# Moving the second batch's scaling layer into the first batch's wide attention

## The chip, the cores and the metric

The kernel runs on one core of one Trainium2 chip. The metric is the device time of one execution in microseconds, median over runs. Five engines work side by side from their own instruction queues and meet through semaphores: TensorE (PE) multiplies, VectorE (DVE) and ScalarE (ACT) do elementwise work, GpSimd (POOL) does elementwise work and issues indirect DMAs, and SyncE (SP) issues the other DMAs.

## The reference

An activation x of 2 batches x 512 tokens x 256 features goes through twelve sublayers, each a layer norm, a block and a residual sum. The last four matter here:

```python
x = x + 0.5 * _L2_ffn_ref(_layernorm(x, axis=-1), ...)   # second routed FFN: top 2 of 8 experts and a shared FFN
x = x + 0.5 * _L3_ffn_ref(_layernorm(x, axis=-1), L3_ffn_weight, L3_ffn_bias)   # scaling layer
x = x + _L3_attn_ref(_layernorm(x, axis=-1), L3_attn_W_Q, ..., L3_attn_W_O)     # wide attention
x = x + 0.5 * _L3_ffn_ref(_layernorm(x, axis=-1), L3_ffn_weight, L3_ffn_bias)
```

The scaling layer multiplies the normed x by a 256 x 256 matrix quantized to -1, 0 and 1 and adds a bias. The wide attention has 16 causal heads of 128 features over each batch.

## The kernel before, in words

Each sublayer of each batch is a unit: unit u is sublayer u // 2 of batch u % 2. Units 16 and 17 are the second routed FFN (MOE2), 18 and 19 the first scaling layer (FFN3), 20 and 21 the wide attention (ATT3), 22 and 23 the second scaling layer. Every engine walks the units in order by a program written out by hand. PE_OF, ACT_OF and DVE_OF name each engine's function for a unit, and SP and POOL have their own lists at the end of the file.

Products keep nearly full precision by splitting each operand into a high part (written by ACT or POOL) and a low part (the difference, written by DVE or POOL), and by three matmuls for one (mm3, lines 282 to 284). So each result that feeds a product passes through ACT and then DVE before PE can use it.

A layer norm is a chain over four engines: dve_stats (four bn_stats, four bn_aggr, small tensor_scalars), pool_ln (a power for the inverse root; for the units in NORM_ACT a second small product), the norm itself on DVE (dve_norm) or, for the units in NORM_ACT, on ACT (act_norm), pe_T (eight transposes into two PSUM banks), act_T and dve_T (high and low part of the transposed x).

The routed FFN handles both batches in one loop of 30 tiles (15 of each batch). SP loads tiles of gathered tokens into raw (m_xs) and stores results in DRAM; POOL gathers each token's two result rows back by eight indirect DMAs of a batch (pool_gather_y) into four slots in raw (m_gath), and DVE adds them to x (dve_combine, two instructions for each of four token tiles). Batch 0 is combined while batch 1's tiles are still multiplied. Batch 1 (unit 17) can only be gathered once its last tile is stored; its combination stands in dve_ffn3(18).

The order of the stretch that the change touches is this. PE ends the tile loop, multiplies the scaling layer of batch 0 (unit 18), waits for the transposed norm of batch 1, multiplies its scaling layer (unit 19), transposes the norm of unit 20, and begins ATT3 of batch 0 with queries and keys of its first head. DVE adds bias and product of unit 18, combines unit 17 as its gathers land, and then does statistics and norm of unit 19 and of unit 20. POOL gathers, does the small powers, and splits the first pair of heads' weights (pre(20)), which SP loads after unit 17 is done, since raw is shared.

In ATT3 the heads go in pairs. The first and the last pair are written out and the pairs between are a loop. For each head PE fills queries and keys of the next head (ACT copies, DVE takes the low part), transposes the probabilities, multiplies the scores of the next head, the probabilities by the values, and the output product. DVE takes the row minima of the scores (dve_min, L1779), ACT the exponential (L1787), DVE the reciprocal of the sums (dve_rinv, L1796), and POOL multiplies the probabilities by it (pool_norm, L1805). POOL also splits the next pair's weights (pool_chunks, L474 and L476). In before, the statistics of unit 21 stand in DVE's queue after the first head of ATT3 of batch 0.

Of the kernel before, what the change touches and what calls it, by code (L numbers as in the profile page):

```python
# [33 lines left out]
P = 128  # L34
NB = 2
# [76 lines left out]
def build(nc, a, out, stop=N_UNITS):  # L112

    with ExitStack() as ctx:
# [110 lines left out]
        _a, m_b = sublayer_tensors(_m_pad2=([P, 12000], F32), m_b=([P, E * EW], F32R))  # L225
        m_dl = small[:, 32:96].rearrange("p (b i e) -> p b i e", b=NB, i=TT)
# [88 lines left out]

        def dve_stats(v, u, tiles=range(TT)):
# [8 lines left out]
            for i in tiles:  # L325
                v.bn_stats(stats[:, b, i, :], x[:, TT * b + i, :]).then_inc(sem("ln_stats"), 1)  # L326
            if tiles[-1] < TT - 1:
                return
            for i in range(TT):
                v.wait_ge(sem("ln_stats"), TT * u + i + 1)  # L330
                v.bn_aggr(mv[:, b, i, :], stats[:, b, i, :]).then_inc(sem("ln_aggr"), 1)
            v.wait_ge(sem("ln_aggr"), TT * (u + 1))
# [4 lines left out]
        NORM_ACT = (1, 2, 3, 4, 5, 6, 7, 8, 11, 12, 13, 17)  # L337

        def act_norm(s, u):
# [4 lines left out]
            if u >= 2:  # L344
                s.wait_ge(sem("ln_T"), 2 * (u - 1))
# [4 lines left out]
        def dve_norm(v, u, tiles=range(TT)):  # L350
# [5 lines left out]
            if u not in NORM_ACT:  # L356
                v.wait_ge(sem("ln_rstd"), u + 1)
                if positive(2 * (u - 1)):
                    v.wait_ge(sem("ln_T"), 2 * (u - 1))
# [25 lines left out]
        def pool_ln(g, u):  # L385
# [4 lines left out]
            g.wait_ge(sem("ln_veps"), u + 1)  # L390
            g.tensor_tensor(rstd[:, b, :], veps[:, b, :], nhalf[:, :], ALU.pow).then_inc(sem("ln_rstd"), 1)  # L391
            if u in NORM_ACT:
                g.wait_ge(sem("ln_rstd"), u + 1)
# [3 lines left out]
        def T_bank(u):  # L397

            return 2 if u in (14, 18) else 0

        def pe_T(pe, u):
# [4 lines left out]
            pe.wait_ge(sem("ln_xn"), TT * (u + 1))  # L406
            if positive(2 * u):
                pe.wait_ge(sem("ln_lo"), 2 * u)
# [9 lines left out]
        def act_T(s, u):  # L418
# [3 lines left out]
            for c in range(DC):  # L422
                s.wait_ge(sem("ln_T"), 2 * u + c + 1)
# [7 lines left out]
        def dve_T(v, u):  # L431
# [3 lines left out]
            for c in range(DC):  # L435
                v.wait_ge(sem("ln_hi"), 2 * u + c + 1)
# [8 lines left out]
        def pe_ready(pe, u):  # L445

            pe.wait_ge(sem("ln_lo"), 2 * (u + 1))
# [345 lines left out]
        def pe_moe2(pe, u):  # L793
# [131 lines left out]
            for n in range(n0 - 1, n0 + N2 + 2):  # L925
# [10 lines left out]
                if n0 <= n - 1 < n0 + N2:  # L936
                    tile_h(n - 1)
                if n0 <= n - 2:
# [85 lines left out]
        def dve_combine(v, u, part):  # L1024

            b, m = u % 2, MOE2_AT[u] // 2
            for k in range(2):
                a_ = 2 * part + k
                v.wait_ge(sem(f"m_got{a_ % 4}"), 16 * (2 * (2 * m + b) + a_ // 4 + 1))
# [3 lines left out]
                ins = v.scalar_tensor_tensor(out=xt, in0=m_gath[:, a_ % 4, :], scalar=m_w[:, b, part, k:k + 1], in1=xt,  # L1033
# [193 lines left out]
        def pool_gather_y(g, u, half):  # L1227
# [40 lines left out]
        def sp_moe2(sp, u):  # L1268
# [303 lines left out]
        def act_T_next(s, u):  # L1572
            act_T(s, u + 1)


        def pe_ffn3(pe, u):
            b, m = u % 2, F3_AT[u]
# [4 lines left out]
            else:  # L1582
                units_done(pe, u)
# [8 lines left out]
            pe_T(pe, u + 1)  # L1592

        def dve_ffn3(v, u):
            b, m = u % 2, F3_AT[u]

            def bias():
                v.wait_ge(sem("const_in"), 16 * CONSTS)
                for t in range(TT):
                    xt = x[:, TT * b + t, :]  # L1600
                    v.scalar_tensor_tensor(out=xt, in0=bias3[:, :], scalar=0.5, in1=xt, op0=ALU.mult, op1=ALU.add)\
                        .then_inc(sem("f3_bias"), 1)

            def residual():
                v.wait_ge(*since("f3_bias", 4 * (m + 1)))
                dve_residual(v, u, 0.5, [("f3_out", 2 * m + 1), ("f3_out", 2 * m + 2)])

            if u == 18:
                bias()
                residual()  # L1610
                for t in range(TT):
# [1218 lines left out]
```

## Time and profile before

| what | us |
|---|---|
| median of 3 runs | 1260.48 (1258.39 to 1263.32) |
| the profiled execution's own time | 1263.04 |
| its span in the trace | 1261.2 |
| mean granted TensorE clock | 0.94 of full speed |
| busy: PE, DVE, ACT, POOL | 1091.8, 849.2, 609.0, 558.2 |

The span is what the trace shows from the first instruction to the last; 1.8 us lie around it. A granted clock of 1.00 is 2.4 GHz and 0.50 is 1.2 GHz. Times of rows are microseconds from the start of the span.

### The profile page before, as it was taken

The page shows a single profiled execution, that of the slowest core. Times are in us where ns is not written, and L with a number is a line of the kernel's source. Part 1 is how long each engine was busy: PE and PEld are TensorE (multiplying, and loading weights), DVE is VectorE, ACT ScalarE, POOL GpSimd, SP SyncE. Part 2 cuts the span into 40 slices and gives each one's busy share as a digit, 9 for nine tenths or more (in the row PEclk, how much of TensorE's full clock was granted, in tenths as well). Part 3 has the DMA queues.
Part 4 walks back from the last instruction along what each step waited for, and adds up shares of the span by engine and source line. Part 5 has one row for each costly group of instructions (what it writes and reads, how often), then busy time and mean ns, then how long its engine had stood idle before and what let it go on. Part 6 is the DMA issues. An engine that isn't in the chain of part 4 may idle for free.

```text
span 1261.2 us, 21660 instructions
## 1 busy us (share of the span) xinstructions
PE 1091.8 (87%) x6545; PEld 936.6 (74%) x6545; DVE 849.2 (67%) x2302; ACT 609.0 (48%) x1434; POOL 558.2 (44%) x666
## 2 busy tenths in 40 slices
PE   5887478999779989988989998992899998999995
PEld 4776367778557779867767777981799997899995
DVE  4577766778977756668768876565656565665666
ACT  2455734321114345567758754550455554555552
POOL 5576618750345440254524438124344442444430
PEclk9898879999889999989989997995899998999998
DMA  5125212230013033322512123432101010010100
GB/s 171 63 66 219 87 68 83 77 113 10 1 62 120 1 114 116 115 76 66 161 34 46 24 80 101 125 112 69 44 26 50 25 50 26 26 50 25 48 2 34
DMA packets 48450, 87.85 MB, mean 70 GB/s; under 512 B 9648, under 2 KB 28464, under 8 KB 47920
## 3 DMA queue, kind: packets, MB, share of 16 engines
q1 hardware_dynamic: 41232, 70.17, 17.5%
q0 software_dynamic: 5120, 13.83, 3.6%
q10 hardware_dynamic: 2016, 2.83, 0.6%
q8 instruction: 43, 0.70, 0.2%
q14 instruction: 39, 0.32, 0.1%
HBM read 61.24 MB, written 19.27 MB: 64 GB/s over the span
## 4 chain that ended last, share of the span: by engine, by line
PE 59%; DVE 21%; ACT 9%; issue 7%; POOL 3%; DMA 1%; SPq 0%; DVEq 0%; another core or an unknown queue 0%; POOLq 0%; ACTq 0%
PE ps L282 18%; PE ps L283 16%; PE ps L284 16%; PE ps L1818 4%; DVE a_ptl L1842 3%; DVE a_p L1779 2%; ACT a_p L1787 2%; ACT a_pth L1834 1%; PE ps L415 1%; DVE x L1560 1%; PE ps L856 1%; DVE stats L326 1%; DVE ffn_hf L726 1%; PE ps L875 1%; DVE ffn_hl L730 1%
## 5 line engine op out<-in xcount | busy, mean ns | idle before, releaser
L1805 POOL TENSOR_SCALAR a_p<-a_p,small 128x128 f32<-128x128 f32 (+3 forms) x256 | 132.6, 537 | 233.5 <-DVE small L1796 233.3
L1787 ACT ACTIVATE a_p<-a_p,small 128x128 f32<-128x128 f32 (+3 forms) x256 | 141.5, 554 | 74.6 <-DVE small L1779 72.4
L1842 DVE TENSOR_TENSOR a_ptl<-ps,a_pth 128x384 fp32r<-128x384 f32 (+1 forms) x192 | 106.6, 596 | 62.7 <-ACT a_pth L1834 62.2
L282 PE MATMUL ps<-xh,wh 128*128 128x512 f32 x304 | 126.3, 416 | 10.1 <-POOL wl L507 5.8
L283 PE MATMUL ps<-xl,wh 128*128 128x512 f32 x304 | 122.8, 404 | 0.0
L284 PE MATMUL ps<-xh,wl 128*128 128x512 f32 x304 | 122.4, 403 | 0.0
L1834 ACT ACTIVATE a_pth<-ps 128x384 fp32r<-128x384 f32 (+1 forms) x192 | 90.4, 523 | 57.6 <-PE ps L1818 57.5
L1779 DVE CUSTOM_DVE_ANT_0 a_p<-ps,maskrow 128x128 f32<-128x128 f32 (+3 forms) x256 | 111.6, 483 | 5.0 <-PE ps L284 2.1
L391 POOL TENSOR_TENSOR rstd<-veps,nhalf 128x4 f32<-128x4 f32 x24 | 25.2, 1051 | 160.8 <-DVE veps L335 160.8
L476 POOL TENSOR_TENSOR wl<-raw,wh 128x1024 fp32r<-128x1024 f32 (+1 forms) x66 | 91.9, 1392 | 5.5
L1818 PE MATMUL ps<-ident,a_p 128*128 128x128 f32 x640 | 86.6, 284 | 8.3 <-POOL a_p L1805 4.2
L282 PE MATMUL ps<-m_a,xh 128*128 x240 | 84.1, 350 | 4.8 <-DVE xl L1157 1.7
L474 POOL TENSOR_SCALAR wh<-raw 128x1024 fp32r<-128x1024 f32 (+1 forms) x66 | 46.7, 708 | 82.5 <-PE ps L284 82.3
L1818 PEld LDWEIGHTS ps<-ident,a_p 128*128 128x128 f32 x640 | 73.7, 146 | 11.4 <-POOL a_p L1805 5.5
L282 PEld LDWEIGHTS ps<-xh,wh 128*128 128x128 f32 x304 | 59.0, 194 | 25.4 <-POOL wl L507 7.7
L283 PE MATMUL ps<-m_b,xh 128*128 x240 | 73.3, 305 | 0.0
L284 PE MATMUL ps<-m_a,xl 128*128 x240 | 73.2, 305 | 0.0
L1238 POOL DMA_INDIRECT raw<-moe_y,m_pos x32 | 31.6, 986 | 91.1 <-DMA moe_y<-m_y 65.6
L415 PE MATMUL ps<-ident,xn 128*128 128x128 f32 x176 | 27.8, 310 | 49.2 <-issue 31.6
L284 PEld LDWEIGHTS ps<-xh,wl 128*128 128x128 f32 x304 | 58.8, 193 | 14.5
L1560 DVE SCALAR_TENSOR_TENSOR x<-ps,small,x 128x256 f32<-128x256 f32 x128 | 61.7, 482 | 8.6 <-PE ps L284 2.2
L283 PEld LDWEIGHTS ps<-xl,wh 128*128 128x128 f32 x304 | 58.9, 194 | 10.9
(368 smaller groups left out, 3438.3 us busy)
## 6 DMA issues: line engine op xcount, KB each, us to landing
raw<-in_w SPq DMA_DIRECT2D x32, 384.0 KB
raw<-in_qk SPq DMA_DIRECT2D x16, 512.0 KB
raw<-moe_x SPq DMA_DIRECT2D x60, 128.0 KB
moe_y<-m_y SPq DMA_DIRECT2D x60, 128.0 KB
m_raw<-in_ex SPq DMA_DIRECT2D x8, 608.0 KB, 7.7
m_raw<-in_ex POOLq DMA_DIRECT2D x8, 608.0 KB, 4.2
raw<-in_v SPq DMA_DIRECT2D x16, 256.0 KB
moe_x<-drh SPq DMA_DIRECT2D x8, 480.0 KB
```

The source lines that it names most:

```text
L282: pe.matmul(o, l[0], r[0], start=start, stop=False, skip_group_check=True)
L283: pe.matmul(o, l[0], r[1], start=False, stop=False, skip_group_check=True)
L284: return pe.matmul(o, l[1], r[0], start=False, stop=stop, skip_group_check=True)
L474: g.tensor_scalar(oh, raw[:, p, at:n], 1.0, 1.0, ALU.mult, ALU.mult).then_inc(sem("w_hi"), 1)
L476: g.tensor_tensor(ol, raw[:, p, at:n], f32(oh), ALU.subtract).then_inc(sem("w_split"), 1)
L1560: v.scalar_tensor_tensor(out=xt, in0=ps[:, 2 + t, e * D:(e + 1) * D], scalar=w_moe1[:, t, 2 * k + e:2 * k + e + 1], in1=xt, op0=ALU.mult, ...
L1779: v.tensor_tensor_reduce(p[:, par, P_AT[i]:P_AT[i + 1]], ps[:, bank, at:at + KEYS[i]], maskrow[:, T - KEYS[i]:T], 1.0, -NEG, ALU.add, ALU.min,
L1787: s.activation(p[:, par, P_AT[i]:P_AT[i + 1]], p[:, par, P_AT[i]:P_AT[i + 1]], ACT.Exp, bias=h_nmx[:, par, i:i + 1], scale=scale, accum_ou ...
L1805: g.tensor_scalar(pp, pp, h_inv[:, par, i:i + 1], 1.0, ALU.mult, ALU.mult).then_inc(sem("at_norm"), 1)
L1818: last = pe.transpose(ps[:, banks[f], at:at + P], p[:, par, P_AT[i] + kb * P:P_AT[i] + (kb + 1) * P], ident[:, :])
L1834: s.activation(dst, ps[:, bank, 0:cols], func, **how).then_inc(sem("at_fhi"), 1)
L1842: ins = v.tensor_tensor(dst, ps[:, bank, 0:cols], f32(hi), ALU.subtract)
```

## The change

- Unit 18's product (now pe_scale3(18)) goes into the tile loop of the routed FFN, ahead of the last tile's down product. ATT3 of batch 0 comes next: transposes, ACT copy and DVE low part of unit 20 stand where unit 19's stood. Unit 20's norm moves from DVE to ACT, and so does unit 19's.
- Unit 17's gathers get a buffer of their own (m_late, eight slots), with no wait for slots; they come after unit 20's small powers in POOL's queue. Its combination stands in the first pair of ATT3 on DVE: tiles 0 and 1 between minima and reciprocal of the first head, tiles 2 and 3 around the next head's query split.
- Unit 19 (statistics, powers, norm, transposes, split, bias, product, residual) goes into the first pair of ATT3, with its transposes in banks 6 and 7. The first head's output product moves behind it, and the statistics of unit 21 move one head later.
- The first pair's weights are loaded by SP inside the routed FFN's loop, before its last two stores; the high part is written by ACT and the low part by DVE in place of POOL.
- The semaphore counts of the layer norms follow the new order (LN_AT). The final store of batch 1 is cut into two halves.

The core of the diff:

```diff
+        LN_AT = {u: u for u in range(N_UNITS)} | {20: 19, 19: 20}
-        NORM_ACT = (1, 2, 3, 4, 5, 6, 7, 8, 11, 12, 13, 17)
+        NORM_ACT = (1, 2, 3, 4, 5, 6, 7, 8, 11, 12, 13, 17, 20, 19)
...
+                if m == 1 and n == n0 + N2 + 1:
+                    pe_scale3(pe, 18)
                 if n0 <= n - 2:
                     tile_down(n - 2, at.pop(n - 2))
...
-                if 2 * TT * q + c >= 4:
+                if u < 17 and 2 * TT * q + c >= 4:
                     g.wait_ge(*since("m_comb", 2 * TT * q + c - 3))
-                g.indirect_dma_start(out=m_gath[:, c % 4, :], out_offset=None, in_=ys[b][:, :],
+                g.indirect_dma_start(out=m_late[:, c, :] if u == 17 else m_gath[:, c % 4, :], out_offset=None, in_=ys[b][:, :],
...
+                if m == 1 and n == n0 + N2:
+                    sp.wait_ge(*since("t_x", n0 + N2))
+                    sp.wait_ge(sem("x_res0"), 4 * 9)
+                    sp.wait_ge(*since("sh_lo", SH_CH * 2 * NB))
+                    for p in range(2):
+                        sp_chunks(sp, 20, 0, p)
...
+        def act_ffn3(s, u):
+            if u == 18:
+                for p in range(2):
+                    n, r = chunk_cols(20, p), RAW0[20] + p
+                    s.wait_ge(sem(f"w_raw{p}"), 16 * (RAW0[20] // 2) + 16)
+                    s.activation(wh[:, p, 0:n], raw[:, p, 0:n], ACT.Copy).then_inc(sem("w_hi"), 1)
+                act_norm(s, 20)
+                act_T(s, 20)
...
         def dve_ffn3(v, u):
             if u == 18:
+                dve_bias3(v, 18)
+                dve_residual3(v, 18)
+                dve_stats(v, 20)
+                for p in range(2):
+                    n = chunk_cols(20, p)
+                    v.wait_ge(sem("w_hi"), RAW0[20] + p + 1)
+                    v.tensor_tensor(wl[:, p, 0:n], raw[:, p, 0:n], f32(wh[:, p, 0:n]), ALU.subtract)\
+                        .then_inc(sem("w_split"), 1)
+                dve_T(v, 20)
...
@@ pe_att3, first pair @@
+                    if side and first and hh == 1:
+                        pe_T(pe, side)
                     pe_transpose_p(pe, n + hh, hh, a3_p, [bank["p", hh, f] for f in range(3)],
                                    [starts["p", hh, f] for f in range(3)])
+                    if side and first and hh == 1:
+                        pe_scale3(pe, side)
                     if not done:
                         scores(n + (hh + 1), at["k", hh, 0] + 1)
+                    if side and first and hh == 1:
+                        units_done(pe, u)
+                        out_head(0, at["z", 0, 0] + 1, start=True)
...
@@ act_att3, first pair @@
+                    if u in SIDE and first and hh == 1:
+                        act_T(s, SIDE[u])
...
+                    if u in SIDE and first and hh == 0:
+                        act_norm(s, SIDE[u])
...
@@ dve_att3 @@
+                    if side and first and hh == 0:
+                        dve_combine(v, 17, 2)
                     if not done:
                         one(("q", hh, 0), a3_ql[:, :], a3_qh[:, :], scale=-SCALE3)
+                    if side and first and hh == 0:
+                        dve_combine(v, 17, 3)
+                    if not done:
                         one(("k", hh, 0), a3_kl[:, :], a3_kh[:, :])
+                    if side and first and hh == 1:
+                        dve_bias3(v, side)
+                        dve_T(v, side)
...
+                    if side and first and hh == 1:
+                        dve_residual3(v, side)
                     if not done:
                         dve_min(v, n + (hh + 1), 1 - hh, a3_p)
+                        if side and first and hh == 0:
+                            dve_stats(v, side)
                         dve_rinv(v, n + (hh + 1), 1 - hh)
                     one(("z", hh, 0), a3_zl[:, :], a3_zh[:, :])
-                    if first and hh == 0:
+                    if first and hh == (1 if side else 0):
                         dve_stats(v, u + 1)
...
             dve_min(v, n0, 0, a3_p)
+            if side:
+                dve_combine(v, 17, 0)
+                dve_combine(v, 17, 1)
             dve_rinv(v, n0, 0)
...
@@ pool_att3, first pair @@
                     if not last:
                         pool_chunks(g, u, r + 1, hh)
+                    if u in SIDE and first and hh == 0:
+                        pool_ln(g, SIDE[u])
...
-            for b in range(NB):
-                sp.wait_ge(sem(f"x_res{b}"), 4 * N_UNITS // 2)
+            for b, t, n in ((0, 0, TT), (1, 0, 2), (1, 2, 2)):
+                sp.wait_ge(sem(f"x_res{b}"), 4 * N_UNITS // 2 - TT + t + n)
...
@@ gpsimd @@
             pool_moe2(g, 16)
+            pool_ln(g, 20)
             pool_gather_y(g, 17, 0)
             pool_gather_y(g, 17, 1)
-            pool_ln(g, 19)
-            pool_ln(g, 20)
-            g.wait_ge(*since("sh_down", SH_CH * 2 * NB))
-            pre(20)
             pool_att3(g, 20)
```

## Rows read from the trace of the kernel before

**Rows 1.** The chain that ended last, 848 to 887 us: start, us, what

```profile
848.30 0.38 PE ps L282
...
850.45 2.14 PE ps L1588 x16
852.59 18.46 issue
...
878.18 4.85 issue
883.03 1.96 PE ps L415 x8
...
886.39 0.80 PE ps L282
```

**Rows 2.** Busy time in windows: PE, PEld, DVE, ACT, POOL, granted clock, DMA share, GB/s

```profile
852.60:858.00 5.40, 0.00 (x0) 0.00 (x0) 1.24 (x3) 0.00 (x0) 3.02 (x4) 0.82 0.17 50
...
890.00:892.00 2.00, 1.17 (x5) 0.65 (x3) 0.84 (x2) 0.77 (x2) 0.00 (x0) 0.95 0.00 0
```

**Rows 3.** DVE in order of time, 848 to 896 us: start, us, instruction

```profile
848.41 1.42 DVE L1601 SCALAR_TENSOR_TENSOR x<-bias,x 128x256 f32<-128x256 f32 x4
851.76 1.62 DVE L459 SCALAR_TENSOR_TENSOR x<-ps,x 128x256 f32<-128x256 f32 x4 [1.94 <-PE ps L1588]
...
874.26 1.40 DVE L326 BATCH_NORM_STATS2 stats<-x 128x6 f32<-128x256 f32 x4
...
895.42 0.08 DVE L1779 DVE_READ_ACCUMULATOR2_ANT small<- 128x1 f32 x1
```

**Rows 4.** POOL in order of time, 854 to 904 us

```profile
854.07 1.01 POOL L1238 DMA_INDIRECT raw<-moe_y,m_pos  x1 [12.17 <-issue]
...
862.96 0.96 POOL L1238 DMA_INDIRECT raw<-moe_y,m_pos  x1 [0.30 <-issue]
...
876.29 1.05 POOL L391 TENSOR_TENSOR rstd<-veps,nhalf 128x4 f32<-128x4 f32 x1 [6.76 <-DVE veps L335]
...
900.49 1.05 POOL L474 TENSOR_SCALAR wh<-raw 128x1024 fp32r<-128x1024 f32 x1 [2.26 <-PE ps L284]
901.62 2.39 POOL L476 TENSOR_TENSOR wl<-raw,wh 128x1024 fp32r<-128x1024 f32 x1
```

**Rows 5.** POOL and ACT in order of time around unit 17's norm

```profile
735.27 0.20 POOL L395 TENSOR_TENSOR nmr<-negm,rstd 128x4 f32<-128x4 f32 x1
...
739.51 2.06 ACT L347 ACTIVATE xn<-x,nmr,rstd 128x256 f32<-128x256 f32 x4
```

**Rows 6.** The experts' weight splits on ACT and DVE: ns min/median/max, first and last start

```profile
L767 ACT ACTIVATE m_a<-m_raw x16: 1199/1202/1222, 383.3 to 759.9; 128x1216 fp32r<-128x1216 f32 x16
...
L772 DVE TENSOR_TENSOR m_b<-m_raw,m_a x8: 1403/1406/1407, 750.1 to 768.4; 128x1216 fp32r<-128x1216 f32 x8
```

**Rows 7.** SP's first weight load of unit 20

```profile
866.77 0.35 SPq L466 DMA_DIRECT2D raw<-in_qk  x1
```

**Rows 8.** The window in which both its pieces were moved, columns as in Rows 2

```profile
868.00:870.00 2.00, 0.00 (x0) 0.00 (x0) 0.74 (x6) 0.00 (x0) 1.04 (x1) 0.50 0.88 341
```

**Rows 9.** PE in order of time, first pair of ATT3, batch 0

```profile
901.81 0.55 PE L1818 MATMUL ps<-ident,a_p 128*128 128x128 f32 x3 [0.65 <-DVE a_kl L1842]
...
915.73 0.33 PE L282 MATMUL ps<-wh,xh 128*128 128x256 f32 x1
```

**Rows 10.** Lines whose DVE instructions read two SBUF tiles: ns min/median/max

```profile
L1723 DVE SCALAR_TENSOR_TENSOR lin_xn<-lin_kv,small x8: 476/710/954, 332.1 to 357.4; 128x256 f32<-128x256 f32 x8
...
L730 DVE TENSOR_TENSOR ffn_hl<-ffn_hf,ffn_hh x32: 691/695/2878, 21.5 to 256.1; 128x512 fp32r<-128x512 f32 x32
```

**Rows 11.** Two windows of PE gaps late in the span, columns as in Rows 2

```profile
1057.00:1058.00 1.00, 1.00 (x9) 1.00 (x8) 0.00 (x0) 0.00 (x0) 0.92 (x2) 0.73 0.00 0
...
1234.00:1236.00 2.00, 0.01 (x1) 0.02 (x1) 1.03 (x3) 1.21 (x4) 1.68 (x4) 1.00 0.00 0
```

**Rows 12.** The final stores, by line

```profile
DMA to landing us min/median/max: 2.9/2.9/2.9
```

More of the change, by code:

```diff
@@ L397, in T_bank @@
         def T_bank(u):
-            return 2 if u in (14, 18) else 0
+            return {14: 2, 18: 2, 19: 6}.get(u, 0)
         def pe_T(pe, u):
@@ L1032, in dve_combine @@
                 xt = x[:, TT * b + part, :]
-                ins = v.scalar_tensor_tensor(out=xt, in0=m_gath[:, a_ % 4, :], scalar=m_w[:, b, part, k:k + 1], in1=xt,
+                ins = v.scalar_tensor_tensor(out=xt, in0=m_late[:, a_, :] if late else m_gath[:, a_ % 4, :], scalar=m_w[:, b, part, k:k + 1], in1=xt,
                                              op0=ALU.mult, op1=ALU.add)
@@ L1591, in pe_ffn3 @@
                     last.then_inc(sem("f3_out"), 1)
-            pe_T(pe, u + 1)
-        def dve_ffn3(v, u):
[L1595 to L1606, printed above, removed]
-            if u == 18:
-                bias()
-                residual()
-                for t in range(TT):
-                    dve_combine(v, 17, t)
+        def pe_ffn3(pe, u):
+            if u == 18:
+                pe_T(pe, 20)
+            if u >= 22:
+                pe_ready(pe, u)
+                units_done(pe, u)
+                pe_scale3(pe, u)
+                pe_T(pe, u + 1)
@@ new lines, in act_ffn3, with dve_bias3 @@
+        def act_ffn3(s, u):
+            if u == 18:
+                for p in range(2):
[4 more added lines that the diff above has]
+                act_T(s, 20)
+            if u == 22:
+                act_T(s, 23)
+        def dve_bias3(v, u):
+            v.wait_ge(sem("const_in"), 16 * CONSTS)
+            for t in range(TT):
+                xt = x[:, TT * (u % 2) + t, :]
+                v.scalar_tensor_tensor(out=xt, in0=bias3[:, :], scalar=0.5, in1=xt, op0=ALU.mult, op1=ALU.add)\
+                    .then_inc(sem("f3_bias"), 1)
@@ L2118, in pair @@
                         qk(1 - hh, [bank["q", hh, 0], bank["k", hh, 0]], [starts["q", hh, 0], starts["k", hh, 0]])
-                    if first and hh == 0:
+                    if side and first and hh == 1:
+                        pe_T(pe, side)
+                    if first and hh == 0 and not side:
                         units_done(pe, u)
-                    else:
+                    if not first or (hh == 1 and not side):
                         out_head(r * 2 + (hh - 1), (base if hh == 0 else at["z", 0, 0] + 1), start=first)
@@ L2148, in act_att3, with pair @@
             b, n0, f0 = u % 2, A3_HEADS[u], A3_FILL[u]
-            def pair(r, last=False):
+            def pair(r, last=False, first=False):
                 fills = pair_fills(last)
@@ L2173, in act_att3 @@
             act_exp(s, n0, 0, -1.0, a3_p)
-            pair(0)
+            pair(0, first=True)
             with s.Fori(1, H // 2 - 1) as r:
@@ L2586, in chunks @@
             def chunks(u):
[L2587 removed]
+                with sp.Fori(1 if u in (0, 20) else 0, CHUNKS[KIND[u]] // 2) as i:
                     for p in range(2):
```

68 lines of the change are left out of this document (35 added, 33 removed).

## The prediction

> **What bounds the kernel now.** I read the chain that ended last first. Between the routed FFN and the wide attention it shows 18.46 us in which PE waits for nothing on its own account, and 4.85 us more after unit 19's product [rows 1]. The timelines of DVE and POOL name what runs meanwhile: gathers of unit 17 one after the other from 854.07, their combination, then unit 19's whole norm, then unit 20's, whose statistics begin at 874.26 [rows 3, 4]. PE's transposes for unit 20 begin at 883.03 and the attention's first product at 886.39 [rows 1]. The windows show PE idle and its granted clock falling on the way; it is back near full only in 890 to 892 [rows 2]. In the attention itself PE is the chain's engine, so time is won by starting it earlier and lost by what is put into it.
>
> **Part 1: the start of the attention.** Unit 18's product takes the place of the last down product. It can start when the down product before has issued: that one starts at 848.30 and is six matmuls of about 0.12, so at 849.0 and not at 850.45 [rows 1], 1.45 earlier. DVE's residual ended at 851.76 + 1.62 = 853.38 behind it [rows 3]; now 851.93. Statistics to the end of the power took 876.29 + 1.05 - 874.26 = 3.08 [rows 3, 4]. The second product on POOL adds its 0.20 [rows 5] and some 0.16 of gaps and one DVE instruction: 855.4. Beside the power DVE splits the low weights. ACT and DVE need 1.20 and 1.40 us for 1216 columns [rows 6], so by width 1.0 and 1.2 for 1024 and about 0.6 and 0.7 for 512. Whether a long DVE instruction holds back POOL's power is not in the trace: nothing, or both pieces (1.9); I take 0.6, since the power's row is of its usual length next to four bias instructions. So 856.0; four ACT norms take 2.06 [rows 5]: transposes start at 858.1, and everything up to the first product keeps its distance, as PE has again been idle and I count on the same low clock. The shift is 858.1 - 883.03 = **-24.9**.
>
> The weights don't delay this. SP loads them after the store of the third last tile, whose down product ends before the one at 848.30 [rows 1]: about 848.1. The two pieces were loaded before from 866.77, and the DMA engines were 0.88 busy in 868 to 870 [rows 7, 8], so they land about 3.4 us later, at 851.5; ACT is free when it has copied the last tile (849.0 + 1.9 for unit 18, 0.7 for the down product, 0.5 for the copy: 852.1) and done with both by 853.7. If they landed as late as 7 us after issue, ACT's norm would still not wait by more than 1. The last two stores go behind these loads in SP's queue and the last down product is 1.9 later, so the gathers start near 856, behind unit 20's power, at (862.96 - 854.07) / 7 = 1.27 apart [rows 4] (eight, 10.2 us). Their last lands about 868. DVE wants the first four at 895.5 - 24.9 = 870.6 (the last minimum ends at 895.5 [rows 3]). POOL is free for the first pool_norm as well. Cost 0, with some 7 us of slack for the first four; beyond that DVE's reciprocal, and behind it POOL, PE and ACT, would wait microsecond for microsecond.
>
> **Part 2: the work put into the first pair**, on the clock of before (subtract 24.9 for the new one). Eight combining instructions at about 0.55 with their waits are 4.4 us on DVE. The first four move the reciprocal from 895.9 to 897.7 and POOL's norm to 900.0, when PE comes to transpose anyway (900.2): free. The other four stand around the query split; without any hindrance the low part of the keys ends at 902.9 and not 901.8, **+1.15** on PE, which waits for just that [rows 9].
>
> But POOL splits the next weights there: 1.05 us from 900.49 and 2.39 from 901.62 [rows 4], and combining reads two SBUF tiles. Two lines of that kind stretch beside POOL's work: 476 to 954 ns and 691 to 2878 ns [rows 10]. So one instruction can lose nothing or up to 2.19. I place the four in time: one behind POOL's last norm (0.6), one or two behind POOL's two pieces. The low keys then end at 906.2, **+3.3** more; bounds 0 and 4.
>
> From there PE's third transpose group runs at 906.2. Scores until 908.6, minima until 909.8. Statistics of unit 19 (1.95) come before the reciprocal; then POOL's two small products (1.4) to 913.2, ahead of POOL's norm of the second head; ACT's norm of unit 19 (2.06) to 915.3, ahead of ACT's copies of queries and keys. PE transposes unit 19 (1.1); ACT copies queries and keys (1.1), DVE takes the low parts by 917.2, adds the bias (1.6 with a short wait) and splits unit 19 (1.3) to 920.1. PE's product takes 1.9, scores 2.0, first output product 1.5, values 1.85: the second pair starts at 927.3. Before it was 915.73 [rows 9]. From the third transposes on that is 21.1 us in place of 13.9, **+7.1**. Of this only 3.0 is PE's own work; the rest is ACT standing before unit 19's norm, and DVE between statistics and split. The statistics of unit 21, one head later, fit into POOL's and DVE's slack: their row cost DVE 2 us in before as well, and POOL's norm in the second pair ends some 0.6 before PE wants it.
>
> **The clock.** In before, PE's clock stayed full in this pair. Now PE has some 5 us with only a few transposes, then two gaps of over 2 us. Late in the span one gap of 2.0 us was followed by a fall to 1.2 GHz (0.73 in 1057 to 1058) and another was not [rows 11]. A fall costs until PE has worked on for a while; from 886.39 to about 890 in before [rows 1, 2], so some 2 us of full-clock work is doubled. I take **+2.3**, bounds 0 and 5.
>
> **Tail.** The last store is halved. It landed in 2.9 us [rows 12]; half the bytes at the 341 GB/s of [rows 8] save 0.7 at most. I take **-0.5**, bounds 0 and -0.8.
>
> **Sum:** -24.9 + 1.15 + 3.3 + 7.1 + 2.3 - 0.5 = -11.5. On the profiled execution's own 1263.04 that is 1251.5. That execution lies 2.6 above the median of the runs, 1260.48; from the median, **1249.0**.
>
> **A rule against the change.** POOL's pieces are the point: [rows 10] give 0.24 for the middle row of the shorter line and 2.19 for the worst of the longer, so four combining instructions would cost 1.0 by the first. The Trainium skill (SBUF — State Buffer, section "Who interferes with whom") says that a VectorE instruction with two SBUF inputs and a GpSimd one that reads SBUF exclude each other, the later waiting for the whole of the earlier. The longest row bears that out, the shortest doesn't tell. By the middle row the sum would be -13.8, by the rule the -11.5 above, and the same rule would let the low-weight split hold back unit 20's power.
>
> **Rivals.**
> - *Power behind the split*: both DVE pieces (1.2 and 0.7) run before POOL's power on the way to the start, 1.3 more than I took: 1250.3. For it: two SBUF inputs on DVE [rows 10]; against it: the power's row at its usual 1.05 [rows 4].
> - *Blocked, but the clock holds*: -13.8, 1246.7. For it: the window at 1234 [rows 11]; against it: the wider gap.
> - *No block*: combining slips between POOL's pieces, PE has no wide gap and the clock holds: -24.9 + 1.15 + 6.8 - 0.5 = -17.5, 1243.0. For it: the shortest times in [rows 10]; against it: POOL's pieces start just there.
> - *The attention doesn't start earlier in effect*: gathers land late and hold the first reciprocal. From 7 us of lateness each microsecond counts; at 12 more the gain is gone, 1255 to 1260. Against it: 1.27 per gather, nothing else in POOL's queue.
> - *Slower*: the granted clock stays at 1.2 GHz through the pair, because its gaps return before PE has worked long enough. Each us of full-clock work done low costs one. Beyond the 2.3 counted, 13.8 us cancel the gain, and 20 make it slower by over 0.5%: 1267. The first pair holds some 26 us of PE work. Against it: every fall in these rows ended after a few us of work [rows 2].
>
> **Chances.** Forecast 0.43; power behind the split 0.08; blocked with full clock 0.16; no block 0.24; late gathers 0.05; low clock throughout 0.04. Anything under 0.5% (6.3 us) can't be told from no change here: below 1254.2 is faster. The first four cases are, but for the forecast's upper end (I give 0.02 of it to no change); late gathers count as no change, the low clock as slower by 0.03 and else as no change. So faster 0.89, no change 0.08, slower 0.03. The range takes the no-block case and a bit of its unused bound (a smaller +6.8), and above it the late power with a second fall of the clock: 1241.5 to 1253.5.
>
> **What the next profile would show.** Transposes of unit 20 some 25 us earlier than 883; if not, the ACT norm or the weights are late, and ACT's row before its high split names which. In the first pair, combining rows stretched beyond 0.48 us or a POOL piece beyond 2.39 for the block; a DVE idle entry on a gather for the late gathers; the granted clock in 1 us windows for the fall. First product to second pair 29.3 us in before, about 43 by my sum, 37 without the block. Wrong would be a pair of under 34 or over 47.

## The result and the profile after

| what | before | after |
|---|---|---|
| median of the runs of one job, us | 1261.53 (4 runs, 1258.39 to 1263.32) | 1248.84 (4 runs, 1246.65 to 1253.06) |
| ratio, 95% interval | | 0.990 [0.988, 0.992] |
| profiled execution: own time, span | 1263.04, 1261.2 | 1253.06, 1251.3 |
| mean granted clock | 0.940 | 0.942 |

Three of the later runs hold one execution in a slow state (2070.19, 1331.33 and 5751.22 us), which is left out of their medians and ratios.

The forecast was 1249.0. How it came out is told best by distances from one mark that both kernels reach by the same code: the start of unit 18's transposes. It lies at 845.25 in the kernel before and at 850.14 in the changed one. In a second profile of the changed kernel (the control, next section) it lies at 845.14, so these 5 us differ from execution to execution and have nothing to do with the change. Rows of PE, kernel before:

```profile
845.25 0.30 PE L415 MATMUL ps<-ident,xn 128*128 128x128 f32 x1
1064.65 0.30 PE L415 MATMUL ps<-ident,xn 128*128 128x128 f32 x1
```

The same of the changed kernel, with the landmarks of the first pair between (unit 20's transposes, first product of the attention, third transposes, unit 19's transposes, second pair); a bracket is the idle time ahead and what ended it. They answer to [rows 1, 9]:

```profile
850.14 0.30 PE L419 MATMUL ps<-ident,xn 128*128 128x128 f32 x1
...
863.48 1.94 PE L419 MATMUL ps<-ident,xn 128*128 128x128 f32 x8 [6.72 <-ACT xn L351]
866.83 0.79 PE L283 MATMUL ps<-xh,wh 128*128 128x512 f32 x1 [1.41 <-DVE xl L447]
...
886.29 0.90 PE L1846 MATMUL ps<-ident,a_p 128*128 128x128 f32 x3 [3.16 <-DVE a_kl L1870]
897.00 1.07 PE L419 MATMUL ps<-ident,xn 128*128 128x128 f32 x8 [1.12 <-issue]
908.52 0.34 PE L283 MATMUL ps<-wh,xh 128*128 128x256 f32 x1
...
1055.31 0.30 PE L419 MATMUL ps<-ident,xn 128*128 128x128 f32 x1
```

Start of each landmark less that of unit 18's transposes in the same profile, us; the runs below are described in the next section:

| profile | unit 20's transposes | first product | unit 19's transposes | second pair | unit 21's transposes | end of span |
|---|---|---|---|---|---|---|
| before | 37.78 | 41.14 | 25.80 | 70.48 | 219.40 | 415.95 |
| after | 13.34 | 16.69 | 46.86 | 58.38 | 205.17 | 401.16 |
| control | 13.35 | 16.70 | 46.91 | 58.39 | 205.13 | 401.06 |
| split after combining | 13.34 | 16.69 | 44.61 | 57.65 | 205.31 | 402.89 |
| bridge in the first pair | 13.33 | 16.69 | 44.93 | 56.41 | 205.35 | 401.24 |
| split by GpSimd | 12.51 | 15.86 | 46.89 | 58.40 | 205.11 | 402.54 |
| before, bridged | 37.86 | 41.21 | 25.89 | 70.44 | 217.12 | 414.27 |
| power first | 13.53 | 16.89 | 46.44 | 57.96 | 204.70 | 400.72 |
| all bridged | 13.34 | 16.69 | 45.08 | 56.61 | 203.37 | 399.61 |
| block, clock, power | 13.55 | 16.90 | 42.89 | 53.56 | 200.25 | 396.73 |
| waits only | 12.51 | 15.86 | 42.42 | 52.98 | 199.71 | 395.62 |
| the same, five bridges | 12.50 | 15.86 | 42.33 | 52.99 | 199.71 | 395.82 |
| eight bridges | 12.38 | 14.99 | 39.12 | 49.77 | 196.51 | 390.87 |

From the mark to the end the change took off 415.95 - 401.16 = 14.8 us: 24.45 won at the start of the attention, 12.35 given back in the first pair (29.3 us from the first product to the second pair before, 41.7 now), 2.1 won between the second pair and unit 21's transposes (148.9 to 146.8), and 0.6 won behind that.

POOL and DVE in order of time say what holds the start, and what holds the first pair; they answer to [rows 3, 4]:

```profile
858.99 1.85 POOL L395 TENSOR_TENSOR rstd<-veps,nhalf 128x4 f32<-128x4 f32 x1 [12.18 <-DVE veps L339]
860.91 0.20 POOL L399 TENSOR_TENSOR nmr<-negm,rstd 128x4 f32<-128x4 f32 x1
...
870.45 0.95 POOL L1245 DMA_INDIRECT m_late<-moe_y,m_pos  x1 [0.30 <-issue]
879.16 2.25 POOL L1833 TENSOR_SCALAR a_p<-a_p,small 128x128 f32<-128x128 f32 x4 [7.76 <-DVE small L1824]
881.50 1.08 POOL L478 TENSOR_SCALAR wh<-raw 128x1024 fp32r<-128x1024 f32 x1
882.66 2.45 POOL L480 TENSOR_TENSOR wl<-raw,wh 128x1024 fp32r<-128x1024 f32 x1
```

```profile
858.75 1.82 DVE L1640 TENSOR_TENSOR wl<-raw,wh 128x1024 fp32r<-128x1024 f32 x2
...
876.08 2.30 DVE L1040 SCALAR_TENSOR_TENSOR x<-m_late,small,x 128x256 f32<-128x256 f32 x4
...
880.20 1.47 DVE L1040 SCALAR_TENSOR_TENSOR x<-m_late,small,x 128x256 f32<-128x256 f32 x2
...
882.44 2.96 DVE L1040 SCALAR_TENSOR_TENSOR x<-m_late,small,x 128x256 f32<-128x256 f32 x2
885.54 0.69 DVE L1870 TENSOR_TENSOR a_kl<-ps,a_kh 128x512 fp32r<-128x512 f32 x1
```

The power takes 1.85 us beside the low split and 1.05 in [rows 4]; that the split holds it back is tested below. Combining takes 0.58 us an instruction where POOL is idle (2.30 for four). The last two take 2.96 together, and 2.38 of that is the second of them alone: it starts at 883.01, behind POOL's second weight piece, and ends at 885.39, just after that piece (885.11). The low part of the keys, for which PE idles 3.16 us, stands right behind them. The last gather is issued at 870.45 and no DVE row waits for it. The windows (columns as in [rows 2], the clock third from the end) show the price of that idle time, and a place where the clock now stays up, at the hand-over between the two attentions:

```profile
884.00:886.00 2.00, 0.00 (x0) 0.00 (x0) 1.85 (x2) 0.00 (x0) 1.11 (x1) 0.69 0.00 0
886.00:888.00 2.00, 1.71 (x8) 1.72 (x9) 1.55 (x4) 0.49 (x1) 0.00 (x0) 0.50 0.75 246
888.00:890.00 2.00, 2.00 (x8) 1.89 (x7) 1.49 (x7) 0.82 (x4) 0.00 (x0) 0.50 0.07 25
890.00:892.00 2.00, 2.00 (x7) 1.59 (x6) 1.29 (x6) 1.30 (x5) 0.00 (x0) 0.60 0.00 0
...
1052.00:1054.00 2.00, 1.16 (x7) 1.03 (x8) 1.20 (x3) 0.94 (x3) 1.92 (x3) 1.00 0.00 0
```

PE idles for 2.0 us ahead of that place in either kernel (first row before, second row changed):

```profile
1056.45 0.38 PE L282 MATMUL ps<-drh,a_zh 128*128 128x256 f32 x1 [2.01 <-DVE a_zl L1842]
1049.29 0.39 PE L283 MATMUL ps<-drh,a_zh 128*128 128x256 f32 x1 [2.02 <-DVE a_zl L1870]
```

The windows of the kernel before, where the fall began in [rows 11]:

```profile
1059.00:1061.00 2.00, 1.23 (x6) 0.83 (x6) 0.91 (x2) 1.09 (x2) 1.92 (x3) 0.50 0.00 0
1061.00:1063.00 2.00, 2.00 (x7) 1.71 (x8) 0.80 (x2) 0.49 (x1) 1.27 (x1) 0.50 0.68 231
```

### The profile page after: what moved, and what is told of

It reads as the page before. It is cut to its first block, busy times and chain, and to the rows that moved or that the text cites. A ratio compares the mean times of both kernels' runs of the same rounds, so it can differ in the third digit from the quotient of the medians.

```text
span 1251.3 us, 21657 instructions
## 1 busy us (share of the span) xinstructions
PE 1097.6 (88%) x6545; PEld 941.7 (75%) x6545; DVE 845.9 (68%) x2298; ACT 616.0 (49%) x1444; POOL 556.7 (44%) x664
## 4 chain that ended last, share of the span: by engine, by line
PE 54%; DVE 17%; ACT 6%; issue 4%; POOL 3%; DMA 1%; SPq 0%; DVEq 0%; POOLq 0%; ACTq 0%
PE ps L283 16%; PE ps L285 15%; PE ps L284 15%; PE ps L1846 4%; DVE a_ptl L1870 3%; DVE a_p L1807 2%; ACT a_p L1815 2%; ACT a_pth L1862 2%; DVE x L1573 1%; PE ps L860 1%; PE ps L879 1%; DVE stats L329 1%; PE ps L419 1%; POOL raw L1245 1%; PE ps L1595 1%
## 5 line engine op out<-in xcount | busy, mean ns | idle before, releaser
L283 PE MATMUL ps<-xh,wh 128*128 128x512 f32 x304 | 127.1, 418 | 10.5 <-POOL wl L511 6.0
L480 POOL TENSOR_TENSOR wl<-raw,wh 128x256 fp32r<-128x256 f32 (+1 forms) x64 | 88.3, 1380 | 5.3
L1846 PEld LDWEIGHTS ps<-ident,a_p 128*128 128x128 f32 x640 | 72.9, 145 | 14.9 <-POOL a_p L1833 6.0
L478 POOL TENSOR_SCALAR wh<-raw 128x256 fp32r<-128x256 f32 (+1 forms) x64 | 45.7, 713 | 78.5 <-PE ps L285 78.2
L285 PEld LDWEIGHTS ps<-xh,wl 128*128 128x128 f32 x304 | 59.0, 194 | 14.6
L283 PE MATMUL ps<-drh,xh 128*128 (+2 forms) x160 | 61.0, 381 | 2.2 <-DVE x L1573 2.2
L285 PE MATMUL ps<-drh,xl 128*128 (+2 forms) x160 | 59.7, 373 | 0.0
```

The lines of the kernel that those rows point to most:

```text
L283: pe.matmul(o, l[0], r[0], start=start, stop=False, skip_group_check=True)
L285: return pe.matmul(o, l[1], r[0], start=False, stop=stop, skip_group_check=True)
L478: g.tensor_scalar(oh, raw[:, p, at:n], 1.0, 1.0, ALU.mult, ALU.mult).then_inc(sem("w_hi"), 1)
L480: g.tensor_tensor(ol, raw[:, p, at:n], f32(oh), ALU.subtract).then_inc(sem("w_split"), 1)
L1846: last = pe.transpose(ps[:, banks[f], at:at + P], p[:, par, P_AT[i] + kb * P:P_AT[i] + (kb + 1) * P], ident[:, :])
```

## The experiments

Medians are of the runs of one job and go with the ratio to the kernel before in that job; the chips of the jobs differ by some us, so jobs are compared by ratios. Small differences are read from the table of landmarks. In the expectations "unit 19's low keys" are the low part of the second head's keys, which PE waits for ahead of unit 19's work, and where the run with the power first speaks of unit 19's transposes as the mark, unit 18's are meant.

**Control: the changed kernel again.**

> The changed kernel as it is, beside which the others of this job are read. Both theories: about 1249 us, about 0.990 of the kernel before; from the end of unit 19's low keys to the second pair a clock of 0.50 for some 5 us.

1248.42 us, ratio 0.989 [0.987, 0.991]; every landmark within 0.1 us of the first profile. The gain from mark to end, 14.9 us, repeats, and this execution has none of the 5 us ahead of the mark.

**GpSimd's split after the combining.**

```diff
@@ pool_att3, first pair, before pool_chunks @@
+                    if u in SIDE and first and hh == 0:
+                        g.wait_ge(*since("m_comb", 8 * TT))
```

> GpSimd's first chunk of the next pair's weight split, inside the first pair of the second attention, waits until the last VectorE product of the combining is done; nothing else changes. Theory (GpSimd's split of 2.45 us holds back the combining's two-input products, and so unit 19 behind them): the product that took 2.96 us takes about 0.7, unit 19's low keys are ready about 2.3 us earlier after unit 20's first product (17.1 instead of 19.4 us), and the time falls by 2.3 to 3 us against the changed kernel, by up to 2 more if the shorter idle time keeps TensorE's clock from falling. Rival (no block: the products are late for another reason): the product keeps its 2.9 us and the time stays within 0.5 us. Second rival (the split, now later, makes the second pair's weights late): the time rises by 1 us or more, and the second pair's first matmul waits for the split.

1247.61 us, ratio 0.987 [0.985, 0.989]. DVE and POOL:

```profile
878.38 1.06 DVE L1040 SCALAR_TENSOR_TENSOR x<-m_late,small,x 128x256 f32<-128x256 f32 x2
879.59 0.69 DVE L1870 TENSOR_TENSOR a_kl<-ps,a_kh 128x512 fp32r<-128x512 f32 x1
```

```profile
879.53 1.05 POOL L478 TENSOR_SCALAR wh<-raw 128x1024 fp32r<-128x1024 f32 x1 [2.18 <-DVE x L1040]
```

The two take 1.06 and not 2.96 us: the block is real, and the row is 1.9 longer for it. The third transposes come 17.9 us behind the first product and not 19.5; the other 0.4 went ahead of the combining, where PE's clock came back 5.1 us behind the first product and not 4.4. Unit 19's transposes come 2.3 us earlier, since the clock still falls behind the key split but is back after some 3 us and not 7. But only 0.7 of that reaches the second pair: the clock falls again in front of unit 19's product, and once more, as briefly, at the hand-over. PE doesn't wait for the later weight split at the second pair. The time can't be told from the control's. The windows behind the key split and in front of unit 19's product:

```profile
881.00:883.00 2.00, 2.00 (x10) 1.90 (x10) 1.66 (x7) 0.83 (x4) 2.00 (x1) 0.54 0.00 0
883.00:885.00 2.00, 2.00 (x7) 1.60 (x6) 1.29 (x5) 1.37 (x6) 0.04 (x1) 0.60 0.45 70
...
894.00:896.00 2.00, 1.36 (x7) 1.36 (x8) 2.00 (x4) 0.00 (x0) 0.00 (x0) 0.71 0.18 69
896.00:898.00 2.00, 2.00 (x11) 2.00 (x11) 0.86 (x3) 0.00 (x0) 0.00 (x0) 0.50 0.00 0
```

**A bridge over the idle time in the first pair.** Transposes whose result nobody reads.

```diff
@@ pe_transpose_p, behind the second group of the first head @@
+                if isinstance(n, int) and n == A3_HEADS[20] and f == 1:
+                    pe.wait_ge(sem("x_res0"), 4 * 10)
+                    for _ in range(24):
+                        pe.transpose(ps[:, 6, 0:P], ident[:, :], ident[:, :])
```

> 24 transposes of the identity, whose results nobody reads, are added on TensorE behind the second group of transposes of the first head, where it idled for about 3.2 us before unit 19's low keys; the rest of the work is the same. Theory (the fall of the granted clock to 0.50 behind that idle time costs 2.3 us of the 42 us from unit 20's first product to the second pair): the clock stays at 1.00 or near it from the third transposes on and the time falls by about 2 us. Rival (the slower matmuls there are hidden by waits for VectorE and ScalarE): the clock stays high as well, but the stretch keeps its 42 us and the time is within 0.7 us of the changed kernel.

1248.75 us, ratio 0.989 [0.987, 0.991]. The clock stays at 1.00 through the pair and the second pair starts 2.0 us earlier, as the theory says. Unit 21's transposes do not: at the hand-over, where the control has 1.00, this profile has

```profile
1044.00:1046.00 2.00, 1.61 (x8) 1.21 (x6) 0.36 (x1) 0.95 (x2) 2.00 (x2) 0.50 0.00 0
```

and from the second pair to unit 21's transposes it needs 148.9 us, just what the kernel before needed, and not 146.7. So both of my statements were too simple: the fall costs 2.0 us where it is, and a second fall took them back.

**The first pair's weights split by GpSimd again.** Placed behind unit 20's small products; ACT's and DVE's loops are gone.

```diff
@@ gpsimd @@
             pool_ln(g, 20)
+            g.wait_ge(*since("sh_down", SH_CH * 2 * NB))
+            pre(20)
             pool_gather_y(g, 17, 0)
```

> The first pair's weights are split by GpSimd again, high and low part, behind unit 20's mean-and-scale work and ahead of the gathers; everything else stays at its new place. Theory (the gain comes from unit 20's place, and the division of the split is worth little): GpSimd needs 4 x about 1.05 to 2.4 us for the split, so TensorE's first product comes about 4 to 6 us later than in the changed kernel, of which VectorE's combining gives some back because it no longer runs against ScalarE and VectorE's split; time +3 to +5 us. Rival (the first product has slack, since unit 19's low keys are the wait that ends last): time within 1 us of the changed kernel, and the low keys stand where they stood.

1251.07 us, ratio 0.991 [0.989, 0.993], not to be told from the control. The theory is refuted: the first product comes 0.84 us earlier, and not 4 to 6 later. That it has slack, as the rival says, shows from the other side: nothing of the 0.84 is left at the second pair.

```profile
853.72 1.01 POOL L395 TENSOR_TENSOR rstd<-veps,nhalf 128x4 f32<-128x4 f32 x1 [12.20 <-DVE veps L339]
854.81 0.20 POOL L399 TENSOR_TENSOR nmr<-negm,rstd 128x4 f32<-128x4 f32 x1
854.97 1.05 POOL L478 TENSOR_SCALAR wh<-raw 128x1024 fp32r<-128x1024 f32 x1
856.10 2.35 POOL L480 TENSOR_TENSOR wl<-raw,wh 128x1024 fp32r<-128x1024 f32 x1
...
859.12 1.27 POOL L480 TENSOR_TENSOR wl<-raw,wh 128x512 fp32r<-128x512 f32 x1
```

POOL's split fits between the power and the first product (860.72): the norm, the transposes and their two parts take that long. The power is back at 1.01 without DVE's split beside it. The gathers start 4 us later and still nobody waits for them. The second pair comes at the same 58.4. Of the 0.84, some 0.4 is gone before PE has the first head's keys, because its clock came back 5.4 us behind the first product (4.4 in the control); the block (2.96 again) and a fall of the same length follow, and the rest goes there. The 1.5 us more at the end lie in the last pair of the second attention, where the clock fell in this profile (0.50 from 1221 to 1224.5) and not in the control's.

**The kernel before with a bridge.**

```diff
@@ pe_att3, last pair, ahead of the output product @@
+                    if last and hh == 1:
+                        pe.wait_ge(sem("at_nmx"), (n + 1) * TT + 2)
+                        for _ in range(14):
+                            pe.transpose(ps[:, 3, 0:P], ident[:, :], ident[:, :])
```

> The kernel before, with 14 transposes of the identity whose results nobody reads added on TensorE in the last pair of either wide attention, where it idled for 2.0 us ahead of the last head but one's output product; all else as before. Theory (part of the change's gain, 2.2 us at the hand-over between the two attentions, is the granted clock, which fell to 0.50 there in the kernel before and not in the changed one): the clock at the hand-over stays at 1.00 and the stretch from unit 20's first product to the second attention's transposes gets about 2.2 us shorter, 178.3 to about 176 us; time about 0.998 of the kernel before. Rival (the matmuls at the lower clock there are hidden by other waits): the clock stays up and the stretch keeps its length within 0.5 us.

1264.06 us against 1267.39, ratio 0.9978 [0.9966, 0.9991]. The clock stays at 1.00:

```profile
1058.00:1060.00 2.00, 2.00 (x18) 1.76 (x16) 0.00 (x0) 0.29 (x1) 1.92 (x2) 1.00 0.00 0
```

The stretch from the first product to unit 21's transposes goes from 178.3 to 175.9 us. So the 2.1 us that the change shows at the hand-over, some 140 us behind the first pair, are a fall of the clock that the profile of the kernel before has and both profiles of the changed kernel happen not to have; the old kernel can have them too.

**The power first.**

```diff
@@ dve_ffn3(18), before the low split @@
+                v.wait_ge(sem("ln_rstd"), LN_AT[20] + 1)
```

> VectorE's low split of the first pair waits until GpSimd's power for unit 20's scale (128 x 4 elements) is done. Theory (the power took 1.85 us because VectorE's split came first): the power takes 1.05 us again, unit 20's transposes start 0.8 us earlier after the last point in common (12.5 instead of 13.3 us behind unit 19's transposes) and the low split, 1.8 us, still ends before the first product wants it; time down by 0 to 0.8 us, the rest lost behind. Rival (the power's 1.85 us has another reason): it keeps them and nothing moves.

1252.16 us, ratio 0.989 [0.987, 0.991]. Unit 20's transposes came 0.2 us later, not 0.8 earlier, and POOL and DVE show why:

```profile
858.53 1.01 POOL L395 TENSOR_TENSOR rstd<-veps,nhalf 128x4 f32<-128x4 f32 x1 [12.19 <-DVE veps L339]
859.61 1.24 POOL L399 TENSOR_TENSOR nmr<-negm,rstd 128x4 f32<-128x4 f32 x1
```

```profile
859.57 1.83 DVE L1641 TENSOR_TENSOR wl<-raw,wh 128x1024 fp32r<-128x1024 f32 x2 [1.18 <-POOL rstd L395]
```

The power is free, and now the small product behind it is held back, 1.24 in place of 0.20: DVE's first piece starts 0.04 us ahead of it and ends at 860.80, and the product ends at 860.85. Right mechanism, wrong cure.

**Bridges at the hand-over too.** The 24 transposes of the first pair and the 14 of the last pair, in the changed kernel.

> The 24 transposes in the first pair of the run before, and 14 more of the same kind in the last pair of either wide attention, where TensorE idled for 2.0 us. Theory (the 2.0 us that the 24 transposes gave until the second pair were taken back by a fall of the clock at the hand-over between the attentions): now the clock stays at 1.00 there too, and the end comes 2.0 us earlier than in the changed kernel, about 1246.5 us. Rival (something other than the clock, DMA or a fixed wait, sets the hand-over): the hand-over still comes 205 us behind unit 18's transposes and the time stays at 1248.5 us.

1252.09 us in a job whose kernel before took 1267.39: ratio 0.987 [0.985, 0.989]. The 2.0 us now live on: second pair at 56.61, unit 21's transposes at 203.37, 1.8 ahead of the control. The interval overlaps the control's; the landmarks carry the verdict.

**Block, clock and power together.** The wait on the combining, the wait on the power, bridges, and DVE's order in the first pair:

```diff
@@ dve_att3, first pair @@
                     if side and first and hh == 1:
-                        dve_bias3(v, side)
                         dve_T(v, side)
+                        v.wait_ge(sem("ln_xn"), TT * (LN_AT[side] + 1))
+                        dve_bias3(v, side)
```

> The changed kernel with GpSimd's first split behind the combining, the power ahead of VectorE's low split, VectorE's rest of unit 19's transposes ahead of the bias instead of behind it, and transposes of the identity, whose results nobody reads, in five idle stretches of TensorE (8, 8 and 10 in the first pair, 14 in the last pair of either attention). Theory (the held-back combining costs about 2.3 us, the power 0.8, the bias about 1, the clock up to 2, each on the path that sets the end): 4 to 6 us less than the changed kernel, 1243 to 1245 us, with a granted clock of 1.00 from the second pair on. Rival (what one wait gives, the next takes): less than 2 us.

1247.16 us, ratio 0.985 [0.983, 0.987]. From mark to end 396.7 us, 4.3 less than the control, as the theory has it, and the clock is at 1.00 from the attention's first scores to unit 23's transposes. Unit 19's transposes come 2.2 us ahead of those in the run with bridges alone (the block), and from there to the second pair it takes 10.7 us in place of 11.5 (the bias).

**Waits only.** No bridges. The wait on the combining and DVE's order are those shown above. In DVE's low split the wait is for both of POOL's small products:

```diff
-                v.wait_ge(sem("ln_rstd"), LN_AT[20] + 1)
+                v.wait_ge(sem("ln_nmr"), NORM_ACT.index(20) + 1)
```

> The changed kernel with three changes of order and no added work: VectorE's low split waits for both of GpSimd's small products for unit 20 (power and the product with the mean), GpSimd's first split waits for the end of the combining, and VectorE takes unit 19's transposes ahead of the bias. Theory: unit 20's transposes come 12.5 us behind unit 18's (13.35 in the changed kernel, 13.53 where only the power went first), the low keys 2.4 us earlier behind the first product, the second pair about 0.85 us earlier behind unit 19's transposes: 4 us in all at the second pair if the clock does not fall in between, 2 to 2.5 if it does. Rival (the split, wherever it stands, holds back the next thing on GpSimd's queue that matters): unit 20's transposes stay at 13.3 to 13.5 us.

1243.12 us, ratio 0.984 [0.981, 0.987]: below the changed kernel's 0.990 and 0.989, with no work added.

```profile
854.35 1.01 POOL L395 TENSOR_TENSOR rstd<-veps,nhalf 128x4 f32<-128x4 f32 x1 [12.20 <-DVE veps L339]
855.43 0.20 POOL L399 TENSOR_TENSOR nmr<-negm,rstd 128x4 f32<-128x4 f32 x1
856.12 1.66 POOL L1245 DMA_INDIRECT m_late<-moe_y,m_pos  x1 [0.49 <-issue]
```

```profile
877.00:879.00 2.00, 0.55 (x3) 0.31 (x3) 1.75 (x5) 0.90 (x2) 0.76 (x1) 1.00 0.00 0
```

Both small products have their own length and unit 20's transposes come at 12.51. The instruction behind them, the first gather, now takes 1.66 us beside the low split (1.02 in the changed kernel, where it comes after the split); nobody waits for it. The second pair starts 5.4 us ahead of the control: 0.8 at the first product, 1.8 more up to the third transposes (the block), 1.9 from there to unit 19's transposes, 0.9 behind them (the order). The 1.9 is the clock, which stayed at 1.00 in the first pair (the window shown) as at the hand-over. That the waits hold it up is not shown: the run with the split after the combining has one of them and its clock fell.

**The same with the five bridges.**

> The run with the five bridged stretches, its low split now waiting for both small products of GpSimd rather than the power alone. Theory: unit 20's transposes at 12.5 instead of 13.55 us, everything behind them 1 us earlier, time 0.8 to 1 us below that run, ratio about 0.984 to the kernel before. Rival: the 1 us is taken up behind the first product, where the combining on VectorE or the gathers end at the same time as before.

1243.06 us, ratio 0.984 [0.982, 0.987], no landmark more than 0.1 from the run without bridges up to unit 21's transposes, the end 0.2 later. In these two profiles the bridges have nothing left to do. Against the run with block, clock and power the theory is about right: unit 20's transposes come 1.05 earlier, the second pair 0.6 and the end 0.9.

**Eight bridges.** 48 more ahead of unit 20's transposes, 18 and 12 in the last two scaling layers.

> The run beside it with transposes of the identity, whose results nobody reads, also in TensorE's idle time ahead of unit 20's transposes (48) and in the last two scaling layers (18 and 12). Theory (the idle time ahead of unit 20 lets the clock fall to 0.50 for some 10 us, in which unit 20's transposes take 1.94 us instead of 1.06 and twelve products 0.43 us each instead of about 0.23): the clock stays at 1.00, the second pair starts 2 to 3 us earlier and the end of the kernel about 1 us more. Rival (VectorE's combining and ScalarE set the pace of the first pair, so faster matmuls only wait longer): the clock is up and the second pair starts less than 1 us earlier.

1238.03 us, ratio 0.979 [0.976, 0.982], the fastest. The clock, 0.50 in 859 to 863 in the run beside it, is 1.00:

```profile
858.00:862.00 4.00, 2.43 (x17) 2.00 (x16) 1.29 (x2) 1.16 (x3) 2.95 (x4) 1.00 0.77 294
```

The second pair starts 3.2 us earlier, a little more than the theory has, and the end comes 4.95 earlier: 1.7 on top, where the theory has about 1.

## Why the prediction was right, point by point

- **Start, forecast -24.9:** the first product came 24.45 us earlier. The steps behind it are seen one by one in the rows, though no run takes one of them out but the split's: norm on ACT at 2.08, transposes behind it. I had given 0.6 to DVE's split on the power; it is 0.84 (13.35 against 12.51 where the split is on POOL or waits for both small products). The rival "power behind the split" thus holds for the first of the two pieces only. That the split went to ACT and DVE at all was worth nothing here.
- **Late gathers:** no row waits for them, not even 4 us later. That rival is out.
- **Combining and block, 1.15 + 3.3 = 4.45:** the low keys end 19.4 us behind the first product and not 15.4, so 4.0. The sum was near and its parts were not. From the first transposes of probabilities to the third it takes 1.57 us before, 4.83 now and 2.94 where the split waits for the combining: so the block behind POOL's weight pieces is 1.9 and not 3.3, and combining without it 1.4 and not 1.15 (two instructions take 1.06 where POOL is idle and 1.47 where POOL's norm runs). The other 0.8 lies ahead of the first transposes, where I had called the first four combining instructions free: PE reaches them 14.6 us behind the first product and not 13.85. 0.2 of it is the clock, back 4.3 us behind the first product and not 3.8; 0.6 are two short waits of PE, for the low part of the values on DVE and for POOL's norm, which the combining has pushed back. Only one instruction lost much to POOL's weight pieces (2.38 for 0.47); I had placed more of them there. "No block" is refuted by the row that goes from 2.96 to 1.06. The Trainium skill (SBUF — State Buffer, section "Who interferes with whom") says that a VectorE instruction with two SBUF inputs contends with a GpSimd instruction that reads SBUF, for a port pair that it calls an exclusive lock. Three rows here agree, in both directions: 2.38 on DVE for a combining instruction of 0.47, and on POOL 1.85 for a power of 1.01 and 1.24 for a product of 0.20. One row doesn't bear out that the later always waits for the whole of the earlier, as the prediction has the rule: the low split's second piece (859.88, with its usual 0.69) ran inside the last microsecond of the power. One after the other the two pieces (1.22 and 0.69) and the power would have ended at about 861.5, and the power ended at 860.84.
- **Third transposes to second pair, 7.1 and 2.3 for the clock:** 22.2 us in place of 13.9, so 8.3 and not 9.4. The clock's part is 2.0 by the bridge, so the chain's is 6.3 and not 7.1.
- **First product to second pair:** 43 forecast, 41.7 measured, inside the 34 to 47 that I had named. The rival "blocked, but the clock holds" didn't come about; the run with the bridge has it, and there it is 39.7.
- **Tail, -0.5:** from the last transposes to the end 10.5 before, 10.0 after: -0.55. No run halves the store alone, so that this is the store is not shown.
- **Not in the sum:** -2.1 at the hand-over. I had read the fall at 1057 and used it as a model for the first pair, and did not ask whether it would be there in the changed kernel. With it the steps add up to 14.8 and not 11.5: on the profiles the forecast was 3.3 short, 2.1 by this, 1.5 by the first pair being shorter and 0.1 by the tail, less 0.45 at the start.
- **The time:** 1249.0 against medians of 1248.84 and 1248.42. That the number fits better than the sum is luck: I subtracted from the median of three runs of before, 1260.48; with the fourth run that median is 1261.53, and in the later jobs it was 1263 to 1267.4. By ratio the change gives 1.0 to 1.1%, 12.7 to 14.6 us.
- **Slips in the working:** 21.1 less 13.9 is 7.2 and not 7.1; "no block" takes 6.8 for that term and doesn't say why; and in "slower" the 13.8 us that cancel the gain include the 2.3 already counted and don't come beyond them.

Open: why the clock fell at a given gap in one profile and not in another. The gap at the hand-over is 2.0 us in the kernel before, in the control, in the run with the split after the combining and in the run with the first bridge; the clock fell behind it in all of these but the control. The same gap at the end of the second attention was followed by a fall in two of the profiles (the split after the combining, the split by GpSimd) and not in the control's. The price of a fall is shown: 0.9 to 1.6 us for the shorter ones (some 3 us long), 2.0 to 2.2 for the longer ones (some 7). What decides whether the clock falls is not.

## What to carry to other kernels

- When side work is put into the idle time of engines that are off the critical path, look for the long instructions that can hold back a short, urgent one on another engine: here two waits and one change of order, with no work added or removed, gave 3.5 us at the second pair on top of the whole move, and 1.9 more in a profile in which the clock happened to hold.
- A wait must cover every urgent instruction on the other engine, not the first one: the hold-up moves to the next, and does no harm once the next is one for which nobody waits.
- Before a small gain or loss is put down to an edit, compare the granted clock in every idle gap of both profiles, also far behind the edit: a fall cost 0.9 to 2.2 us here, and the single edits gave 0.8 to 1.9.

## What was not expected of the hardware

- A DVE instruction that began 0.04 us ahead of a POOL instruction of 0.20 us on 4 columns held it for a microsecond; size doesn't protect.
- With work nobody reads in PE's idle time, PE's clock stayed at 2.4 GHz in every stretch so filled up to the last scaling layers: unit 20's eight transposes took 1.04 us in place of 1.94, and the kernel 4.75 us less than with the waits alone from the mark to the end (395.62 to 390.87), 5.1 by the medians of that job (1243.12 to 1238.03).
